# Attention stage of a graph network: exponentials placed ahead of the node matrices on ScalarE, and PSUM split four and two instead of three and three

## The reference, cut to what matters

```
feat   = xl[src] + xr[dst]
feat   = where(feat >= 0, feat, 0.2 * feat)
logits = einsum('ehc,hc->eh', feat, att)
ex     = exp(logits - segment_max(logits, dst)[dst])
alpha  = ex / (segment_sum(ex, dst)[dst] + 1e-16)
out    = segment_sum(alpha[:, :, None] * xl[src], dst)
```

## Time and profile before

| | |
|---|---|
| median of 3 runs | 2502.48 us (2498.19 to 2504.38) |
| profiled execution | 2508.43 us |
| its span, first to last instruction | 2506.6 us |
| mean granted TensorE clock | 0.886 |
| busy: PE, PEld | 1984.4 us, 1690.5 us |
| busy: DVE, POOL, ACT | 1516.3 us, 1214.0 us, 1191.0 us |
| first and last start of the logits' products (L1139) | 181.0 and 1660.4 us |

### The profile page before, as it was taken

How to read it: one execution, slowest core, us unless ns; L and a number is a source line. 1 busy time by engine, 2 the same in 40 slices (tenths; PEclk the granted TensorE clock), 3 DMA queues, 4 the chain that set the end, 5 groups by cost and what they waited for, 6 DMA issues and landing times. The chain is left out here.

```text
span 2506.6 us, 43475 instructions
## 1 busy us (share of the span) xinstructions
PE 1984.4 (79%) x9692; PEld 1690.5 (67%) x9693; DVE 1516.3 (60%) x3638; ACT 1191.0 (48%) x2805; POOL 1214.0 (48%) x1207
## 2 busy tenths in 40 slices
PE   2974788878888888878888888887886626999996
PEld 2763666767777676767676776667875525888885
DVE  5964777777777777777778777788456440111110
ACT  2542555555555555555555555655545412232321
POOL 3346656555666556655656565520002551344444
PEclk9988998998989899998989899988985557999998
DMA  7675666666666666666666666626602335666664
GB/s 210 228 250 180 193 186 195 185 188 183 194 187 188 180 189 191 194 182 188 189 184 195 176 191 187 190 68 188 204 7 90 108 120 166 136 145 141 144 143 76
DMA packets 256713, 422.34 MB, mean 168 GB/s; under 512 B 45802, under 2 KB 128089, under 8 KB 256653
## 3 DMA queue, kind: packets, MB, share of 16 engines
q1 hardware_dynamic: 154608, 223.36, 28.4%
q0 software_dynamic: 65408, 153.31, 24.9%
q10 hardware_dynamic: 36636, 45.00, 5.6%
HBM read 358.65 MB, written 62.86 MB: 168 GB/s over the span
## 5 line engine op out<-in xcount | busy, mean ns | idle before, releaser
L822 POOL DMA_INDIRECT ring<-xl_rows,a_idx x928 | 890.5, 960 | 594.1 <-issue 272.4
L1139 PE MATMUL a_f_ps<-a_xr_w,a_hot_n 128*128 128x256 f32 x1856 | 571.4, 391 | 177.1 <-DVE a_pos L997 77.8
L1141 PE MATMUL a_f_ps<-ring,ident 128*128 128x256 f32 x1856 | 591.3, 402 | 0.4 <-issue 0.4
L1139 PEld LDWEIGHTS a_f_ps<-a_xr_w,a_hot_n 128*128 128x128 f32 x1856 | 368.0, 203 | 280.5 <-issue 165.1
L1154 PE MATMUL a_o_ps<-ring,a_hot_e 128*128 128x264 f32 x1856 | 535.3, 415 | 19.4 <-issue 13.4
L1154 PEld LDWEIGHTS a_o_ps<-ring,a_hot_e 128*128 128x128 f32 x1856 | 377.0, 207 | 94.0 <-issue 26.5
L997 DVE SCALAR_TENSOR_TENSOR a_pos<-a_f_ps,att_cols 128x512 f32<-128x512 f32 x464 | 316.2, 681 | 190.8 <-remote 120.9
L903 ACT ACTIVATE a_hot_e<-a_far_e,one 128x512 f32<-128x512 f32 x232 | 167.6, 723 | 444.0 <-PE a_o_ps L1154 247.2
L1007 DVE TENSOR_REDUCE a_lg<-a_pos 128x8 f32<-128x512 f32 x464 | 316.0, 681 | 25.2 <-remote 14.9
L1021 DVE TENSOR_TENSOR ring<-ring,a_sm_ps (+1 forms) x464 | 315.2, 679 | 1.7 <-issue 1.7
L1141 PEld LDWEIGHTS a_f_ps<-ring,ident 128*128 128x128 f32 x1856 | 305.6, 202 | 1.2 <-issue 1.1
(11 more groups left out here) (349 smaller groups left out, 2206.3 us busy)
## 6 DMA issues: line engine op xcount, KB each, us to landing
a_xr_w<-xr_rows SPq DMA_DIRECT2D x464, 256.0 KB
a_rel_bc<-rel_rows ACTq DMA_DIRECT2D x116, 256.0 KB
x_w<-in_L_ffn_W_dram SPq DMA_DIRECT2D x57, 512.0 KB, 4.2
ring<-xl_rows,a_idx POOLq DMA_INDIRECT x928
xr_rows<-xr_parts SPq DMA_DIRECT2D x50, 256.0 KB, 2.1
ring<-disp_rows SPq DMA_DIRECT2D x49, 257.0 KB
xl_rows<-xl_sb SPq DMA_DIRECT2D x50, 132.0 KB, 1.8
j_xl<-xl_rows SPq DMA_DIRECT2D x25, 264.0 KB, 2.9
```

The costliest lines, as they stand in the source:

```text
L822: nc.gpsimd.indirect_dma_start(xl_e[:, p * T + 2 * h + u, :], None, k.xl_rows, bass.IndirectOffsetOnAxis(ap=idx[:, p, 2 * h + u:2 * h + u ...
L1139: nc.tensor.matmul(f_ps[:, slot(h), u, :], hot_n[:, j % 2, 2 * g + u, :], xr_w[:, h % XR, a, :].bitcast(F32R), start=(a == 0), stop=False)
L1141: last = nc.tensor.matmul(in_heads(f_ps[:, slot(h), u, :]), k.ident[:, :], heads_of(xl_e[:, p * T + 2 * h + u, :])[:, :, 0:C], start=False ...
```

## The change

Two edits, both in `attend`. In ScalarE's pass j = 3, `exponents` and `fade_factor` are issued before `near_nodes` and `hot_nodes` instead of after them. And `f_ps` gets four banks, `o_ps` two; a unit takes bank h mod 4 for its logits and h mod 2 for its sums, and each waits for the unit 4 or 2 positions back. No instruction is added or removed.

```diff
-    slot = lambda h: 1 if h == NU - 1 else h % 3
-    freed_by = lambda h: h - (4, 2, 4)[h] if h < 3 else h - 2 if h == NU - 1 else h - 3
+    FS, OS = 4, 2
...
-        f_ps = pb("a_f_ps", [P, 3, 2, D])
-        o_ps = pb("a_o_ps", [P, 3, 512])
+        f_ps = pb("a_f_ps", [P, FS, 2, D])
+        o_ps = pb("a_o_ps", [P, OS, 512])
...
+                        if soft_in and j == 3:
+                            exponents(c)
+                            fade_factor(c)
                         edges = behind(c, 2 * j + 3, SUM)
...
-                        if soft_in and j == 3:
-                            exponents(c)
-                            fade_factor(c)
...
-                    nc.vector.scalar_tensor_tensor(pos[:, h % 2], f_ps[:, slot(h)], 0.0, att, ALU.max,
+                    nc.vector.scalar_tensor_tensor(pos[:, h % 2], f_ps[:, h % FS], 0.0, att, ALU.max,
...
-                    nc.vector.tensor_tensor(at, o_ps[:, slot(hh), 0:XW], at, ALU.add).then_inc(added, 1)
+                    nc.vector.tensor_tensor(at, o_ps[:, hh % OS, 0:XW], at, ALU.add).then_inc(added, 1)
...
-                    wait_past(pe, settled, c * NU + (freed_by(h) + 1))
+                    wait_past(pe, settled, c * NU + (h - FS + 1))
...
-                    wait_past(pe, added, cc * NU + (freed_by(hh) + 1))
+                    wait_past(pe, added, cc * NU + (hh - OS + 1))
```

More of the change, by code:

```diff
@@ L1135, in logits_of @@
                     pe.wait_ge(landed[h % LANDS], c * (32 * NU // LANDS) + (h // LANDS + 1) * 32)
-                    wait_past(pe, settled, c * NU + (freed_by(h) + 1))
+                    wait_past(pe, settled, c * NU + (h - FS + 1))
                     for u in range(2):
                         for a in range(PARTS):
-                            nc.tensor.matmul(f_ps[:, slot(h), u, :], hot_n[:, j % 2, 2 * g + u, :], xr_w[:, h % XR, a, :].bitcast(F32R),
+                            nc.tensor.matmul(f_ps[:, h % FS, u, :], hot_n[:, j % 2, 2 * g + u, :], xr_w[:, h % XR, a, :].bitcast(F32R),
                                              start=(a == 0), stop=False)
-                        last = nc.tensor.matmul(in_heads(f_ps[:, slot(h), u, :]), k.ident[:, :],
+                        last = nc.tensor.matmul(in_heads(f_ps[:, h % FS, u, :]), k.ident[:, :],
                                                 heads_of(xl_e[:, p * T + 2 * h + u, :])[:, :, 0:C], start=False, stop=True)
@@ L1151, in sums_of @@
                     pe.wait_ge(msg_ready, cc * NU + (hh + 1))
-                    wait_past(pe, added, cc * NU + (freed_by(hh) + 1))
+                    wait_past(pe, added, cc * NU + (hh - OS + 1))
                     for u in range(2):
-                        last = nc.tensor.matmul(o_ps[:, slot(hh), 0:XW], hot_e[:, j % 2, 2 * g + u, :],
+                        last = nc.tensor.matmul(o_ps[:, hh % OS, 0:XW], hot_e[:, j % 2, 2 * g + u, :],
                                                 xl_e[:, pp * T + 2 * hh + u, :], start=(u == 0), stop=(u == 1))
```

## The result

The changed kernel takes 2484.84 us (median of 5, 2480.45 to 2486.69) against 2502.48 (2496.99 to 2504.71). The ratio is 0.9933 [0.9915, 0.9951]: it is 17 us faster (12 to 21). The forecast was 40 us faster. Measured again (e5, chip 6), it gives 0.9937 [0.9922, 0.9953].

A forecast was written before the change was run, and what follows sets the result against it. No engine is full; they wait for each other, with GpSimd's loop and held signals limiting gains. Order -26 and banks -14 give -40 us: 2508.4 to 2468.4 profiled, 2462.5 median; own range 2440 to 2480, whole range 2415 to 2540.

The forecast's parts named there:

- The stalls aimed at: TensorE's idle time ahead of the logits' products (L1139), 177.1 us, and ahead of the turn of the weights (L1172), 109.0.
- the turn's delay over 0.84 us: Time from L1081's end to the turn's start beyond the least seen: 38.1 us over 27 chunks, 32.6 removable.
- wait for `settle` at positions 15 and 1: TensorE's logits wait for banks freed two positions earlier: about 2.2 and 1.9 us a chunk; four banks remove the cause.
- the signs named for being wrong: GpSimd's runs become twos, rounds past 3.2 us; or VectorE idles more before `add_up`; or logits' unit times and 51 us stay.
- the gain at TensorE itself: Bank edit, waits around positions 15 and 1: 1.1 us less at each, 2.2 us a chunk, 62 us over 28.
- the pass-through: Share of removed TensorE stalls becoming time: 0.8 of 32.6 for the order (-26 us), a quarter for the banks (-14).
- GpSimd's round of 3.13 us a unit: GpSimd's loop of gathers and waits for signals: 3.14 and 3.13 us a unit, limiting gains from the kernel's 3.20.
- the fourth bank frees TensorE wholly: Rival at TensorE: sums rarely bind and both parts count in full, -95 us, 2407; chance 0.14.
- two banks starve VectorE: Rival in held stretches: VectorE runs dry sooner, GpSimd sees two units per round, +33 us, 2536; chance 0.27.
- the time is given back: Rival: the turn comes earlier but everything waits for the next signals; both edits within 10 us of nothing, 2495 to 2510; chance 0.14.
- the forecast's explanation: GpSimd issues gathers in unbroken runs, 1.26 us each; TensorE's signals from a run's later part arrive together after it stops.
- signals are held: TensorE's signals reach VectorE, ScalarE and GpSimd late; a sum through at 530.60 was taken by VectorE at 535.87.

The follow-up runs named there:

- e5: The changed kernel once more, nothing altered, against the kernel before on chip 6: ratio 0.9937.
- e2: The kernel before with only the banks changed (four for logits, two for sums), exponentials left behind the node matrices: ratio 0.9988 to the kernel before.
- e1: The kernel before with only the ScalarE order changed (exponentials ahead of the node matrices), three banks each: ratio 0.9927 to the kernel before.
- e3: The changed kernel with a third sum bank, one softmax bank, and messages reading weights from the ring in SBUF: ratio 0.9894 to the kernel before.
- e4: The changed kernel with one softmax bank and messages reading weights from the ring in SBUF, eighth bank idle: ratio 0.9892 to the kernel before.
- e10: The changed kernel with every fourth unit's second gather replaced by a plain SyncE load (other rows): 2311 us, ratio 0.9312 to the kernel before.
- e16: The changed kernel with every fourth unit's second gather loaded by SyncE, run where signals come on time: ratio 0.9768 to the kernel before.
- e7: The changed kernel with each unit's second gather replaced by a same-size plain SyncE DMA (other rows): 2135.9 us, ratio 0.8536 to the kernel before.
- e9: The kernel before with each unit's second gather replaced by a same-size plain SyncE DMA (other rows): 2127.7 us, ratio 0.8576 to the kernel before.
- e14: The changed kernel once more, run where the kernel before takes near 2156 us: ratio 1.0002 to the kernel before.
- e11: The kernel before with exponentials ahead and messages reading weights from the ring in SBUF, two softmax banks kept: ratio 0.9889 to the kernel before.
- e17: The kernel before, unchanged, run for its trace where signals come on time: ratio 1.0001.
- e6: The changed kernel without each unit's second gather after the first 32 units: 2169.8 us, ratio 0.8667 to the kernel before.
- e15: The kernel before with exponentials ahead and messages reading ring weights, run where signals come on time: ratio 1.0284 to the kernel before.

## Why the forecast was wrong in size

*The stalls aimed at: found rightly, removed as said.* Over chunks 2 to 28 the turn's delay over 0.84 us fell from 38.1 us to 4.8, where 32.6 was called removable. The fade factor ended 0.60 us after its argument in the median (24 of 27 below 0.75). In e2, without the new order, that delay is 49.5. The wait for `settle` at positions 15 and 1 is gone. The idle time ahead of the turn fell further than said (18.2, not near 80), and what came up ahead of the sums is larger than what went ahead of the logits (+196 against -125), where "smaller" was forecast. Of the signs named for being wrong, one came true: the logits' unit times stay (391 and 392 ns in L1139's line) and the chunk still takes 50.7 us, near the 51.

*The step that failed for the banks comes first: the gain at TensorE itself.* The prediction worked out 2.2 us a chunk, 62 us, by pricing the sums around positions 14 to 0 and 5 and leaving every other position as it was. In e2, counted by position over 25 chunks, the waits around 14 to 1 did shrink, from 4.1 us a chunk to 1.8, and those at 5 and 6 from 0.8 to 0.6. But ahead of the sums of positions 3, 4 and 9 to 13 TensorE now waits 2.7 us a chunk, where it had waited 0.2. Ahead of logits and sums together it waits 5.3 us a chunk before and 5.3 in e2 (and 8.2 in the kernel after): nothing was gained there. With two banks TensorE can run less far ahead of VectorE at every position, and the prediction had looked at three.

*The other step that failed is the pass-through, the share of a removed stall that becomes time.* For the order edit it said 0.8 of 32.6, -26 us; measured alone it is -18 (-13 to -23), 0.6 of the 30.5 us between the turn's delay before and in e1 (38.1 to 7.6, on two chips). For the banks it said a quarter of 62, -14; measured alone it is -3 (-8 to +2). Together they gave -17, not -40. VectorE's idle time fell by 0.4 us a chunk, not by 1 to 1.5. The forecast had GpSimd's round of 3.13 us a unit beside the kernel's 3.20 and priced the slack between them as nearly free. It is not: the pace is what GpSimd needs per gather with its pauses, and that went from 1.60 us to 1.58. From the 101st gather to the last takes 1322.9 us before and 1306.8 after; the gathers themselves take 793 us in both, and the pauses (over 0.45 us between gathers) went from 331 us to 308. There are 23 pauses fewer (153, from 176), each replaced by an ordinary gap of 0.30 us, and that is the whole gain.

*The rivals.* That the fourth bank frees TensorE wholly is out: it is worth 3 us. That two banks starve VectorE is out too: GpSimd's runs became longer (5.3 gathers in the mean, from 4.6), 79% of the gathers are now in runs of six, that is of three units, where 31% were, and a third bank (e3) adds nothing to e4. That the time is given back is what the runs show, nearly whole for the banks and in part for the order. The 17 us measured lie outside its "within 10 us of nothing" all the same.

*What set the price.* Shown: time follows the number of gathers in both places (e10, and e16 down to VectorE's 38.8 us), the stall ahead of the sums comes and goes without it (e3 against e4), and both edits are worth nothing that shows once the loop is lightened (e7 against e9) or signals are on time (e14). Also seen: between 330 and 1600 us GpSimd pauses 170 times before, 169 in e2, 144 in e1, 150 after and 111 in e11, about 2 us each. The banks leave the number of pauses as it was (e2), the order edit lowers it (e1, on e2's chip), and so does reading the ring (e4, on that chip too: 122). Open: why the order edit lowers it; which batch of signals the earlier turn joins was not traced. Open too: what holds TensorE's signals at all, and whether it is the chip or the time of the run that decides. The kernel before took 2480 us on chips 3 and 15, 2502 on chip 6 and 2156 on chips 9 and 11, on chip 11 twice; but the runs on 9 and 11 were also the last. GpSimd's run was the forecast's explanation. The traces bear it out in part: of VectorE's waits in `settle` and `add_up` that ended over 1 us after TensorE's work (137 before, 140 after), 77 and 101 ended 1.2 to 2.9 us after the end of a run, 11 and 13 inside one. A run alone does not do it: in e14 and e17 none of 47 such waits ended over 0.4 us late. Where signals are held, halving the gathers nearly ends it (6, 2 and 1 waits over 1 us late in e6, e7 and e9). So it seems to take both; no run shows more.

## What to carry to other kernels

Before a stall is priced, ask which loop sets the pace, and test it by taking work from the suspect: GpSimd was busy 48% of the span, as little as ScalarE and less than all others, and halving its gathers took 13 to 15% off, while clearing 216 us of stalls at TensorE, busy 79%, took off 0.7%. When a limited resource such as a bank is moved from one use to another, work out the new waits at every position, not only at those that waited before. A wait that ends on a signal that was itself late moves when its cause is taken away; count it as a gain only if the loop behind it gets shorter too. And an edit tuned where one thing is late should be timed in a second place: here a gain of 0.7% became none, and a gain of 1.1% became a loss of 2.8%.

## What the runs showed that was not expected

- The same kernel takes 2479.6 to 2502.5 us on some chips and 2155.6 to 2156.0 on others, 13 to 14% less, each within 0.5% of its median. GpSimd's and VectorE's instructions have the same lengths in both (a gather 0.96 us, `settle` 0.68). What differs is when TensorE's signals arrive: where VectorE waits for them, 3.6 us after TensorE's work in the mean before, and within 0.4 us in e17.
- When VectorE takes both inputs of the messages from SBUF (e11, e15) instead of one from PSUM, its own instruction stays at 0.68 us, and GpSimd's gathers go from 0.96 to 1.03 or 1.04 us, 7 to 8%.
- TensorE's granted clock rose from 0.91 to 0.96 in the kernel after, though TensorE stood idle longer. In the 25 chunks it was at half speed for 222 us before and for 99 after. Its waits over 3 us went from 34 to 9 while their total grew; that the shorter waits are the reason is likely, but no run tests it.
